# Attention inside a three-layer stack: the weighted values of two units back to back in four slots, and each normalisation one slot later

## The reference, cut to what matters

```
q, k, v = split_heads(x @ Wqkv.T)            # 16 heads, width 32
s  = q @ k.T / sqrt(32)                      # per head 128 x 128
p  = softmax(s)                              # L1: with the mask; L0: times a coherence per head, plus a field term
o  = (p @ v) heads merged
x  = x + o @ Wo.T  (L0: + bias; L1: rms norm and shift first)
```

## Time and profile before

| | us |
|---|---|
| median of 3 runs (3058.72 to 3062.87) | 3061.34 |
| profiled execution | 3061.82 |
| its span, first to last instruction | 3060.1 |
| PE busy | 2926.5 (96%) |
| PEld busy | 2531.9 (83%) |
| DVE busy | 2042.9 (67%) |
| ACT busy | 1367.8 (45%) |
| POOL busy | 705.3 (23%) |

### The profile page before, as it was taken

One profiled execution on the slowest core, in us unless ns is written; L12 is line 12 of the kernel. 1 busy time (PEld: TensorE's weight loads), 2 busy tenths in 40 slices (PEclk: granted clock), 3 DMA queues, 4 the chain that ended last, 5 costly groups with the idle time before them and its releaser, 6 DMA issues. The chain is left out here.

```text
span 3060.1 us, 69590 instructions
## 1 busy us (share of the span) xinstructions
PE 2926.5 (96%) x27253; PEld 2531.9 (83%) x27253; DVE 2042.9 (67%) x3640; ACT 1367.8 (45%) x2219; POOL 705.3 (23%) x562
## 2 busy tenths in 40 slices
PE   6999999998999999988999999599999999999997
PEld 5899999997888888877888888488888888888886
DVE  5777777776788888788877776454444454665554
ACT  3454444544666666555656665332222232222221
POOL 1122222222211111143322332122222221111111
PEclk7999999999999999989999999699999999999999
DMA  3432333344444444534443434521112141111101
GB/s 138 88 86 73 92 86 96 86 97 115 94 101 108 99 106 103 131 92 101 106 110 103 110 103 86 163 69 55 56 55 69 55 147 47 42 45 52 55 28 42
DMA packets 493850, 266.89 MB, mean 87 GB/s; under 512 B 410752, under 2 KB 468224, under 8 KB 493216
## 3 DMA queue, kind: packets, MB, share of 16 engines
q1 hardware_dynamic: 493728, 265.21, 32.9%
HBM read 122.53 MB, written 41.94 MB: 54 GB/s over the span
## 5 line engine op out<-in xcount | busy, mean ns | idle before, releaser
L885 ACT ACTIVATE att_shifted<-att_shifted,keep_lift 128x512 f32<-128x512 f32 x384 | 276.6, 720 | 357.5 <-DVE att_shifted L1034 353.0
L1030 DVE TENSOR_REDUCE att_top<-att_bank_s 128x4 f32<-128x512 f32 x384 | 264.4, 689 | 230.4 <-PE att_bank_s L720 227.7
L1622 DVE TENSOR_TENSOR mlp_act_t<-mlp_bank_u,mlp_sg 128x512 f32<-128x512 f32 x128 | 88.5, 692 | 455.3 <-ACT mlp_sg L1524 451.6
L1664 POOL TENSOR_TENSOR mlp_al<-mlp_act_t,mlp_ah 128x512 fp32r<-128x512 f32 x128 | 175.0, 1367 | 857.5 <-ACT mlp_ah L1530 857.5
L1524 ACT ACTIVATE mlp_sg<-mlp_bank_g 128x512 f32<-128x512 f32 x128 | 76.6, 598 | 630.8 <-PE mlp_bank_u L1437 630.7
L880 ACT ACTIVATE att_pq<-att_shifted 128x512 f16<-128x512 f32 x384 | 240.7, 627 | 160.1 <-DMA att_pt<-att_pq 154.2
L1038 DVE TENSOR_TENSOR att_pq<-att_shifted,att_pq 128x512 f16<-128x512 f32 x384 | 276.9, 721 | 14.0 <-ACT att_pq L880 13.7
L735 PEld LDWEIGHTS att_bank_o<-keep_v,att_pt 128*128 128x128 f16 x7680 | 221.8, 96 | 69.3 <-issue 24.0
L735 PE MATMUL att_bank_o<-keep_v,att_pt 128*128 128x34 bf16 x7680 | 256.1, 178 | 21.6 <-DVE att_of L1060 11.4
L1034 DVE TENSOR_TENSOR att_shifted<-att_bank_s,att_top 128x512 f32<-128x512 f32 x384 | 265.6, 692 | 16.4
L671 PE MATMUL att_bank_a<-att_oth,att_woh 128*128 128x256 f32 x768 | 233.7, 304 | 1.6 <-DVE att_otl L1074 1.5
(11 more groups left out here) (256 smaller groups left out, 8162.7 us busy)
## 6 DMA issues: line engine op xcount, KB each, us to landing
resid<-att_xres SPq DMA_DIRECT2D x47, 512.0 KB, 3.0
mlp_xf<-resid SPq DMA_DIRECT2D x32, 512.0 KB, 4.5
mlp_res<-resid SPq DMA_DIRECT2D x32, 512.0 KB, 4.7
att_xin<-resid SPq DMA_DIRECT2D x31, 512.0 KB, 3.7
att_xres<-resid SPq DMA_DIRECT2D x31, 512.0 KB, 4.2
att_xin<-in_x SPq DMA_DIRECT2D x16, 512.0 KB, 3.9
att_xres<-in_x SPq DMA_DIRECT2D x16, 512.0 KB, 3.7
mlp_yt<-resid SPq DMA_DIRECT2D x16, 512.0 KB, 7.0
```

The source lines that it names most:

```text
L885: nc.scalar.activation(shifted[:, u % 2], shifted[:, u % 2], ACT.Exp, bias=k["lift"][:, 0:1], scale=SCALE).then_inc(exp_done, 1)
L1030: nc.vector.reduce_max(top[:, u % 2, :], bank_s, AX_X).then_inc(top_ready, 1)
L1664: nc.gpsimd.tensor_tensor(al[:, c % 2, :], act_t[:, c % 2, :], f32(ah[:, c % 2, :]), ALU.subtract).then_inc(a_low, 1)
```

## The change

PE calls `weigh_values` for two units in a row in slots 5, 7, 9 and 11 and for none in the others; before, it called it for one unit in each of the slots 4 to 11. DVE calls `normalise` for pairs 0, 1 and 2 in slots 6, 8 and 10 and for pair 3 at the very start of the next body (after the last body, behind the loop); before, they stood in slots 5, 7, 9 and 11.

```diff
--- before.py
+++ after.py
@@ -803,7 +803,8 @@
                         project_pieces(pieces[s])
                     if s < UNITS:
                         scores(i, s)
-                    if s >= 4:
+                    if s in (5, 7, 9, 11):
+                        weigh_values(i, s - 5)
                         weigh_values(i, s - 4)
                     if not at_last:
                         project_pieces(pieces[s])
@@ -1131,6 +1132,8 @@
             def body(i):
                 pieces = pieces_of(i)
                 for s in range(SLOTS):
+                    if s == 0 and positive(i):
+                        normalise(i - 1, 3)
                     if s == 0 and positive(i) and lay(i - 1) == 0:
                         add_field(i - 1, 1)
                     if s < UNITS:
@@ -1151,8 +1154,8 @@
-                    if s in (5, 7, 9, 11):
-                        normalise(i, (s - 5) // 2)
+                    if s in (6, 8, 10):
+                        normalise(i, (s - 6) // 2)
@@ -1198,6 +1201,7 @@
             iterate(dve, body)
+            normalise(ALL - 1, 3)
             low_output(ALL - 1, 1)
```

## The result

The changed kernel takes 3065.71 us (median of 15 runs, 3061.50 to 3072.50), the kernel before 3059.89 in the same series (15 runs, 3053.84 to 3063.85). The ratio is 1.0015, 95% interval 1.0008 to 1.0022: slower, by less than the 0.2% that the prediction set as its border, though the interval reaches just over it. The forecast of 3069.0 is 3.3 us too high; the time lies in the range. The profiled execution took 3068.3, 2.6 above the median of its series, with a span of 3066.5, 6.45 above the span of before.

The account below looks back on a forecast made before the run. PE sets the time in the steady bodies. The terms -7.3 - 2.0 + 12.4 + 3.5 + 0.6 = +7.2 us on the profiled 3061.8 gave 3069.0 us, forecast's own range 3064 to 3074, overall range 3056 to 3077.

Parts of the forecast that it names:

- Layer 0, -0.52 a body: Layer 0: 0.18 from regrouped bursts plus 0.34 from slot 10's wait for pair 2's normalisation; 14 bodies, -7.3 us.
- rival 3: Layer 0 keeps only 0.18 of its 0.52, as slot 11's burst still meets pair 2's normalisation: 3074; chance 0.16.
- Layer 1, -0.14: Layer 1: burst gain of 0.18 a body less 0.04 for scores reaching DVE's subtraction; 14 bodies, -2.0 us.
- Layer 2, +0.89: Layer 2, slot 6: pair 0's normalisation delays the bank read by 0.58, the removed burst gains nothing; 14 bodies, +12.4 us.
- The layer changes, +3.5: Where layers change: three bursts moved behind waits, 0.5 each; later normalisations 0.9, 0.6 and 0.5; could be 0 to +8.
- The last body, +0.6: Last body: pair 0's normalisation enters DVE's chain ahead of the low probabilities that get transposed, +0.6 us.
- The transposes, 0: Even units' buffers free one slot later, but transposes wait longer for their probabilities, so costed at nothing.
- Rival 1: PE-side gain without the loss in layer 2, DVE's order costing nothing there: 3054; chance 0.13.
- Rival 2: Batches as such gain: no loss in layer 2 and none at the layer changes: 3050; chance 0.03.
- Rival 4: No visible effect: layer changes at 0 and the bank read's delay growing by 0.4: 3063; chance 0.13.
- The chances: Against a border of 0.2%, or 6.1 us: faster 0.11, same 0.36, slower 0.53.

Follow-up runs that it names:

- e8: Kernel before with only the burst of unit 6 moved from slot 10 to slot 11, normalisations unmoved: 3052.78 us, ratio 0.9971.
- e1: Changed kernel, but in slot 6 DVE empties the projection bank before it normalises pair 0: 3056.09 us, ratio 0.9988.
- e6: Kernel before with only pairs 2 and 3 changed: bursts of 40 in slots 9 and 11, normalised in slots 10 and 0: 3065.59 us, ratio 1.0017.
- e2: Changed kernel's bursts of 40, with the normalisations back in slots 5, 7, 9 and 11: 3060.68 us, ratio 1.0002.
- e9: On top of e1, in layer 2 DVE empties the projection bank even before it subtracts slot 6's scores: 3044.93 us, ratio 0.9941.
- e12: e10 with bursts of 40 in every body; last three bodies of layers 0 and 1 keep the old normalisations: 3037.65 us, ratio 0.9934.
- e4: Changed kernel, but the last three bodies of each layer keep the bursts and normalisations of before: 3059.78 us, ratio 0.9996.
- e10: e9 and e4 together, with layer 2 in the new order to its end: 3037.41 us, ratio 0.9928.

## Why the prediction was right, and where its steps were off

- **The net result** is close partly by luck, because two errors cancel: layers 0 to 2 came out 4.6 us better than the sum (-9.1, -2.3 and, with its last bodies, +9.9 against -7.3, -2.0 and +12.4), the layer changes 4.5 worse. Another 0.9 was gone before the first body; the kernels differ there by up to 4 (2.0 under before in e8, 1.5 over in e1), which I take for scatter of the first loads. The last body took 0.3 more than its term. Together that is +6.45 against +7.2. Of the 3.3 us by which 3069.0 is too high, 1.9 lie in the starting value, 3061.8, where the kernel before has 3059.89 in this series, and 1.4 in the sum, 7.2 against 5.8 between the medians.
- **Layer 0, -0.52 a body:** measured -0.59. The mechanism was right, and rival 3 falls. e8 moves that burst alone and gets 0.36, of which about 0.27 is the wait that I read as 0.34 from the earlier trace rows; e6, with pairs 2 and 3 alone, gets all but 0.01. What I left out is that the burst which leaves slot 6 needs the new place of pair 0's normalisation: with the bursts alone only 0.08 stays (e2).
- **Layer 1, -0.14:** measured -0.21; no run takes the 0.07 apart.
- **Layer 2, +0.89:** measured +0.99. Step and cause were right (e1, e9). The size was read from the wrong pair: the earlier trace rows are pair 1, 0.58. Pair 0, the one that moves in front of the read, held DVE 0.68 already in slot 5 of the kernel before (DVE's timeline):
```profile
1459.68 0.20 DVE L1045 RECIPROCAL att_rz<-att_bank_o 128x8 f32<-128x8 f32 x1
1460.01 0.42 DVE L1060 TENSOR_TENSOR att_of<-att_bank_o,att_rz 128x256 f32<-128x256 f32 x1
1460.36 0.68 DVE L1038 TENSOR_TENSOR att_pq<-att_shifted,att_pq 128x512 f16<-128x512 f32 x1
```
In the changed kernel it is 0.67. The rest of the term, 0.31 for bursts, is what e1 keeps: 34.80 - 34.48 = 0.32. It depends on the removed burst of slot 6 being worthless, and e9 shows that: once the read is early, a body is under that of before. Over the whole layer the term still came out too large, +9.9 against +12.4: from body 44 to 47 the changed kernel gains 0.9, though two bodies there have the wait at L1006. PE's waits for a transpose in these last bodies fall from 4.4 us to 2.0.
- **The layer changes, +3.5:** measured +8.0 in this profile. This term was mis-sized, and its reasons only half right. I charged three bursts that move behind a wait; e12, which moves two of them (the third, in the first body of layer 2, stood in the new place in all of e4, e10 and e12), shows no cost. The normalisations do it, and from layer 0 to 1, where I had taken 0.5, they cost 1.5 (changed kernel against e4) to 2.4 (e9 against e10, bodies 12 to 18). The wait of 7.0 for pair 0's normalisation did turn, as foreseen, into one for the bank, of 8.4 (at L1002). In e1 and e9 it is 7.6: the read ahead of the normalisation in slot 6 helps here too. From body 29 to 32 a bound on the clock's part can be given. The sums of three stretches, before and after:
```profile
sum 143.80, PE 117.89 PEld 103.27 DVE 111.87 ACT 79.67 POOL 53.08; mean PE 39.30 PEld 34.42 DVE 37.29 ACT 26.56 POOL 17.69
```
```profile
sum 147.00, PE 119.82 PEld 104.19 DVE 109.92 ACT 79.52 POOL 51.57; mean PE 39.94 PEld 34.73 DVE 36.64 ACT 26.51 POOL 17.19
```
Of the 3.2 more, at most 1.9 stand in PE's busy time, where slower matmuls would show; the rest is waiting. For the other part of the 8.0 I can't say.
- **The last body, +0.6:** measured +0.9 from body 47 to the end.
- **The transposes, 0:** PE's waits for them fell from 8.5 us (8 times) to 3.7 (5 times) over the whole span.
- **Rivals 1 and 2** were what the change could have been. Rival 1, no loss in layer 2, needs a read that is not behind the normalisation: e1 is just that, at 3056 where I gave 3054 for it. Rival 2, the Trainium skill's rule on batches, has nothing in the runs for it: bursts of 40 in place of 20 leave the clock at 1.00, and by themselves they bring 1.0002 (e2). Rival 4 falls with both of its conditions: the delay at L1006 grew by 0.67, not 0.4, and the layer changes were not at 0.
- **The chances:** most of mine lay on slower by over 0.2%; the ratio of 1.0015 is inside. The forecast stood just above the border, and the 3.3 us by which it was high decided that.

## What to carry to other kernels

Where the busiest engine does two kinds of work in turn, a piece that you take out of a slot gains its time only if nothing else ends later behind it: look which bank or buffer the next instruction waits for, and when that is released. On the engine that releases it, put the read that frees a shared bank ahead of work that nobody waits for yet, even ahead of the slot's main work if the engine idles there; here that was worth more (21 us from the changed kernel to e9) than the regrouping, which by itself was worth nothing (e2). In written-out bodies at a stage's end, where the busiest engine waits anyway, try the old order by itself: here it gave 7.5 us more (e9 to e10).

## What the runs showed of the hardware

A VectorE instruction on 8 columns can take 2.3 us where it meets GpSimd. The source view of the kernel before, then of the changed one (duration in ns, least, median, most):
```profile
L1050 DVE TENSOR_TENSOR att_rz<-att_rz,att_cf x64: 166/168/2121, 87.7 to 753.0; 128x8 f32<-128x8 f32 x64
```
```profile
L1051 DVE TENSOR_TENSOR att_rz<-att_rz,att_cf x64: 166/168/2332, 91.3 to 749.7; 128x8 f32<-128x8 f32 x64
```
And the timeline of DVE and POOL in the changed kernel, where the longest stands and in a body of layer 0's loop:
```profile
691.49 2.33 DVE L1051 TENSOR_TENSOR att_rz<-att_rz,att_cf 128x8 f32<-128x8 f32 x1
...
691.46 4.66 POOL L102 TENSOR_TENSOR att_wvl<-att_spare,att_wvh 128x1024 fp32r<-128x1024 f32 x2 [9.09 <-ACT att_wvh L97]
...
346.42 1.03 DVE L1051 TENSOR_TENSOR att_rz<-att_rz,att_cf 128x8 f32<-128x8 f32 x1
...
346.04 1.39 POOL L1229 TENSOR_TENSOR att_tl<-att_tf,att_th 128x512 fp32r<-128x512 f32 x1 [3.09 <-ACT att_th L861]
```
The first starts 0.03 behind GpSimd's first subtraction over 1024 columns and lasts as long as that one does (4.66 for two). The second starts 0.38 behind GpSimd's and ends 0.02 behind it, at 347.45 and 347.43. The Trainium skill (SBUF — State Buffer, section "SBUF: two separate sides") calls the pair of ports that the two engines share an exclusive lock: a VectorE instruction with two inputs in SBUF and a GpSimd instruction that reads SBUF can't both have it, and whichever starts first holds it for the whole instruction. This trace agrees, with 2332 and 1030 ns beside a median of 168.

Such meetings are something that the change brings to layer 0: 30 of the 64 instructions take over 0.25 us, where 3 did before, since the normalisations of pairs 0 and 1 now meet GpSimd's `att_tl` in nearly every body. They make up 13.7 us of DVE's busy time between 200 and 650, which is most of its rise from 337.86 to 355.12. PE doesn't pay for them there: e6, which leaves these two pairs in their old slots, has 41.85 a body against 41.84.

The longest one, at 691.49, is part of a normalisation that PE then waits 2.9 for, at the change from layer 0 to 1. In the kernel before that normalisation was over 3 us ahead of GpSimd's start. But two later ones met GpSimd there too, at 702.80 for 1.08 us and at 732.87 for 2.12 us, so the change moves the meetings more than it adds to them. That this one makes up the cost of the layer change is not shown: e4, e10 and e12 put back all the normalisations of those bodies, not this one.
